# Nine row tiles for ACT instead of six, in longer bursts, in the plain aggregation runs of a graph network

## The reference

```
agg  = segment_sum((x @ weight[r])[edge_type, src], dst)          # layer 0
mean = segment_sum(x[src], dst) / max(deg, 1)                     # layer 1
out  = segment_sum(softmax_edges(...)[:, :, None] * feat[src], dst)   # layer 2, three times
out  = segment_sum(h[src] * (dinv[src] * dinv[dst])[:, None], dst)    # layer 3
```

## Time and profile before

| | |
|---|---|
| median of 3 runs | 6626.07 us (6622.88 to 6629.47) |
| profiled execution | 6623.83 us, its span 6622.0 us |
| PE, DVE, POOL, ACT busy | 71%, 68%, 69%, 44% of the span |
| plain runs in the span | a0 from 385 us, a1 from 1353 us, a5 from 5657 us to the end |

### The profile page before, as it was taken

One profiled execution on the slowest core, in us unless ns is written; L12 is line 12 of the kernel. 1 busy time (PEld: TensorE's weight loads), 2 busy tenths in 40 slices (PEclk: granted clock), 3 DMA queues, 4 the chain that ended last, 5 costly groups with the idle time before them and its releaser, 6 DMA issues. The chain is left out here.

```text
span 6622.0 us, 117574 instructions
## 1 busy us (share of the span) xinstructions
PE 4723.6 (71%) x16858; PEld 2807.9 (42%) x16858; DVE 4472.2 (68%) x11788; ACT 2887.8 (44%) x11591; POOL 4600.5 (69%) x4869
## 2 busy tenths in 40 slices
PE   9977777766777657767775777775677677666666
PEld 4445554543333334444443444443444444333333
DVE  5146566555555578888886888886888888655555
ACT  3310000000000067888875888885788888000000
POOL 0057777767777637777776777777777777677776
PEclk9988888878888877888887888787788877777777
DMA  6444444433333345555544555554555554344443
GB/s 204 160 138 122 123 123 122 122 107 109 109 109 109 106 143 141 142 143 144 141 118 135 142 142 146 142 141 148 139 142 141 142 144 118 102 116 116 117 116 106
DMA packets 446609, 865.78 MB, mean 131 GB/s; under 512 B 121901, under 2 KB 273094, under 8 KB 445866
## 3 DMA queue, kind: packets, MB, share of 16 engines
q0 software_dynamic: 227728, 627.54, 34.6%
q1 hardware_dynamic: 174624, 190.99, 9.1%
q10 hardware_dynamic: 43514, 39.73, 2.0%
HBM read 755.74 MB, written 102.10 MB: 130 GB/s over the span
## 5 line engine op out<-in xcount | busy, mean ns | idle before, releaser
L671 POOL DMA_INDIRECT rows_a<-table,rows_src x2454 | 2350.3, 958 | 882.5 <-issue 530.6
L891 PE MATMUL ps<-rows_a,hot_a 128*128 x4980 | 1858.6, 496 | 776.9 <-DMA rows_a<-table,rows_tile_a 407.6
L2064 ACT ACTIVATE rows_a<-rows_a,ex_a 128x64 f32<-128x64 f32 x9588 | 2321.1, 337 | 0.0
L2141 PE MATMUL ps<-rows_a,hot_a 128*128 128x260 f32 x4908 | 1814.3, 490 | 159.4 <-DVE agg L1973 145.9
L806 DVE TENSOR_TENSOR agg<-agg,ps 128x256 f32 (+1 forms) x2490 | 1045.6, 420 | 1202.4 <-PE ps L891 1130.3
L736 POOL DMA_INDIRECT rows_a<-table,rows_tile_a x1460 | 1383.5, 948 | 445.3 <-issue 257.8
L891 PEld LDWEIGHTS ps<-rows_a,hot_a 128*128 128x128 f32 x4980 | 1026.5, 236 | 1533.2 <-DVE agg L806 866.6
L1973 DVE TENSOR_TENSOR agg<-agg,ps 128x260 f32 x2490 | 1038.4, 417 | 319.0 <-PE ps L2141 130.4
L2141 PEld LDWEIGHTS ps<-rows_a,hot_a 128*128 128x128 f32 x4908 | 973.7, 230 | 449.2 <-issue 342.5
L736 POOL DMA_INDIRECT rows_a<-table,row x759 | 721.0, 950 | 231.6 <-issue 151.4
L2076 PE MATMUL ps<-ident,el_a 128*64 128x128 f32 x156 | 57.1, 366 | 520.1 <-DVE fac_a L1960 507.9
(11 more groups left out here) (355 smaller groups left out, 4165.3 us busy)
## 6 DMA issues: line engine op xcount, KB each, us to landing
rows_a<-table SPq DMA_DIRECT2D x6528, 1.0 KB
dstt_a<-dloc_dram SPq DMA_DIRECT2D x156, 512.0 KB
own_a<-table SPq DMA_DIRECT2D x4608, 1.0 KB
table<-ob SPq DMA_DIRECT2D x48, 1024.0 KB, 4.6
rows_a<-table,rows_src POOLq DMA_INDIRECT x2454
rows_a<-table ACTq DMA_DIRECT2D x2304, 1.0 KB
rows_a<-table,rows_tile_a POOLq DMA_INDIRECT x1460, 3.2
table<-ob_n SPq DMA_DIRECT2D x98, 130.0 KB, 3.0
```

The lines of the kernel that those rows point to most:

```text
L671: nc.gpsimd.indirect_dma_start(out=rows[:, n % ring, 0:width], out_offset=None, in_=table, in_offset=bass.IndirectOffsetOnAxis(ap=index[:, ...
L891: nc.tensor.matmul(ps[n % banks][:, 0:width], hot[:, m % nbuf, j, :], mine[n % 4], start=True, stop=True).then_inc(step_done, 1)
L2064: ins = nc.scalar.mul(a, a, ex[:, k % GV, s, h:h + 1])
L2141: nc.tensor.matmul(ps[j % banks][:, 0:W4], hot[:, j, :], step_rows(k, j), start=True, stop=True).then_inc(step_done, 1)
```

## The change

ACT takes every 86th tile from tile 78 on, which makes nine: 78, 164, 250, 336, 422, 508, 594, 680 and 766. Each is asked for in five bursts of 26, 26, 26, 25 and 25 rows. Three bursts stand ahead of the first block instead of four, and one follows each of the blocks 0 to 41. SP's requests for ACT's row numbers are placed by ACT's tile numbers. The constants also go into the step numbering, whose slices are cut from the first such tile on.

```diff
-ACT_TILE = 128
-ACT_FIRST = 100
+ACT_TILE = 86
+ACT_FIRST = 78
 ACT_TILES = tuple(range(ACT_FIRST, T - 1, ACT_TILE))
 ACT_PLACES = 2
-BURST = 16
-BURSTS_AHEAD = 4
+BURSTS = ((0, 26), (26, 52), (52, 78), (78, 103), (103, P))
+BURSTS_AHEAD = 3
...
-                        each = a[:, 0:n * stride].rearrange("p (i e) -> p i e", e=stride)
-                        nc.vector.tensor_scalar(own_tile[:, q, lo:lo + n], each[:, :, at:at + 1].rearrange("p i e -> p (i e)"),
+                        each = a[:, at:at + n * stride].rearrange("p (i e) -> p i e", e=stride)
+                        nc.vector.tensor_scalar(own_tile[:, q, lo:lo + n], each[:, :, 0:1].rearrange("p i e -> p (i e)"),
...
-                        sp.wait_ge(asked, P // BURST * (i - 1))
+                        sp.wait_ge(asked, len(BURSTS) * (i - 1))
...
-                    if ready < len(ACT_TILES) and i == (ACT_TILE * (ready - 1) + ACT_FIRST) // OWN_TILE - 1:
+                    if ready < len(ACT_TILES) and i == ACT_TILES[ready - 2] // OWN_TILE + 2:
...
-                bursts = iter(range(len(ACT_TILES) * P // BURST))
+                bursts = iter(range(len(ACT_TILES) * len(BURSTS)))
...
-                    i, lane = q * BURST // P, q * BURST % P
+                    i, (lane, end) = q // len(BURSTS), BURSTS[q % len(BURSTS)]
...
-                    ask_rows(act, mybir.EngineType.Activation, act_index[:, i % 2], lane, lane + BURST, BURST, octets, 4 * D,
+                    ask_rows(act, mybir.EngineType.Activation, act_index[:, i % 2], lane, end, end - lane, octets, 4 * D,
```

## The result

The changed kernel takes 6700.63 us (median of 5 runs, 6700.08 to 6707.59) against 6626.07 us: ratio 1.0118, 95% interval 1.0107 to 1.0129. It is 1.2% slower, where 0.17% faster was forecast and 6627 us was the end of the range.

What follows compares the result with a forecast made beforehand. POOL's issue of gathers was taken as the bound; 3 fewer gathers in each of three plain runs save 11.3 us, everything else costs nothing: 6626.1 - 11.3 = 6614.8 us, range 6608 to 6627.

Steps and rivals of the forecast that it cites:

- The gain, 11.3 us: POOL issues 3 fewer gathers in each of the three plain runs, each worth about 1.25 us: 11.3 us saved.
- Rival 3: Moved tiles bring nothing, since landings and not issues set the pace: 6626 us, chance 0.07.
- ten more register loads, 0.1 to 1.0 us: In each of ACT's longer bursts, loading ten more row numbers into registers adds 0.1 to 1.0 us.
- ACT's block: ACT's time per block with the new burst: 16.6 to 17.8, 18.6 to 19.6 and 19.0 to 20.0 us by run.
- POOL is reached only beyond ... 20.5 us a block: Ring allowance grows one step per block, so ACT's backlog holds up POOL only beyond 20.5 us a block.
- the last blocks give the backlog back: At a run's end, the last seven blocks, five before, have no burst and give ACT's backlog back.
- The head: ACT's upfront bursts of 78 rows take 3 to 5 us longer; covered by the ring, so no cost taken.
- rival 2: Part of the gain goes: POOL held up at t = 59 or second run ending late, 4 to 7 us; chance 0.14.
- The late number list: Second run, block 37: ACT stands 31 us for its last list of row numbers; nothing lost, bound 2 us.
- Rival 1: Slower: ACT's wait for its number list becomes the second run's end, blocks 37 to 48; 6636 us, chance 0.12.
- gaps over 0.3 us put down to PE: Sign of being wrong: POOL waiting on PE before gathers for longer than the forecast maximum of 0.3 us.
- a longer tail of the second run: Sign of being wrong: the second plain run's tail is longer than before.

Runs made afterwards that it cites:

- experiment 1: Changed kernel with bursts of 28, 28, 24, 24, 24 rows, so loads start on 16 bytes: 6624.46 us, ratio 0.9985 to the kernel before.
- experiment 2: Changed kernel, same bursts, ACT's loads of row numbers widened to start and end on 16 bytes: 6625.39 us, ratio 0.9985 to the kernel before.
- experiment 5: As experiment 1, with SP's requests for ACT's numbers one SP tile earlier: 6625.54 us, ratio 0.9984 to the kernel before.

## Why the prediction was wrong

**The gain, 11.3 us: right.** 3 x 3 gathers at 1.25 us. It shows in experiments 1 and 2 as 0.15% of 6635.54, 10 us, and no gap of POOL put down to PE passes 0.3 us in them. Rival 3, that the moved tiles bring nothing, falls with it.

**"ten more register loads, 0.1 to 1.0 us": the step that failed.** The ten are the numbers by which a load grew, from 16 to 25 or 26. I bounded them by nothing and by the whole gap of 1.5 us between bursts of 16 shared out over its 16 numbers, as if the number of registers were all. It measured 2.1 us in two bursts of five and 5.5 to 5.7 in three (a1), which is 0.9 and 4.3 to 4.5 us more than the 1.2 of before, 3.0 on average. The kernel before holds no load off 16 bytes: its starts are multiples of 16 numbers on ACT and of 32 on SP. Both ends of my bound were rows of the same kind, and the range was blind to the other. The borders 26, 78 and 103 stood in the diff. The Trainium skill, page "Runtime: NRT & Kernel Launch", section "Instruction fetch mechanics", gives about 200 ns a register, without a word on alignment. Its section "The ~15µs preamble/postamble breakdown" describes such loads as coming from HBM. The loads here come from SBUF, and agree with it only off 16 bytes (0.22 us).

**ACT's block, "19.0 to 20.0 us" in the last run and "16.6 to 17.8" in the first: too small.** Measured 21.3 and 20.7. The sum was also slightly off: its own terms give 19.1 to 20.3 us in the last run and 18.7 to 19.9 in the second (18.6 to 19.6 stood there). In a5 the load explains it: 5.6 us on average for 2.6, while the part between root and load was 6.8 us for the 7.7 of the block I read. In a0 the base was wrong as well: that part took 7.6 us on average and 6.4 in the one block I read, since ACT's waits for two of PE's products there grew from 1.2 and 1.6 us to 2.0 and 1.9; the load took 4.2 us for 1.2.

**"POOL is reached only beyond ... 20.5 us a block": roughly right, and not the edge that mattered.** POOL got gaps in a0 (20.7) and a5 (21.3), and none over 0.3 us in a1 (19.9). With two slow loads it had some 5 us of them already at 20.1 in a0 and 20.6 in a5. But the end of the run pays earlier, from 19.8 to 20.1 us: six intervals without a burst give back 11.0 us in place of 19.3 in a5, 50 us, and 12.6 in a0, 40 us, and the longer head has used some of that. I wrote that the last blocks give the backlog back and did not say up to which block length; that sum is the one to make. It comes close and no more: with the first root 3.0 us (a5) and 7.4 us (a0) later, it puts the edge at 20.4 and 20.1 us, 0.3 above what the table gives, and I can't place the rest.

**The head, "3 to 5 us longer": too small.** 78 rows took 34.0 to 34.5 us where 64 took 26.2, one of the three loads being slow. With good loads (experiment 2) they took 30.1 to 30.3, 4 us more, as forecast. "I take nothing" was not quite so: the first gaps of the changed kernel's a0 stand ahead of tiles 60 and 62, where the prediction looked for them (rival 2), but they exceed 0.3 us by 0.8 us together.

**The late number list, 31 us in the second run, "nothing lost": right, with the wait too long.** It is some 21 us in experiment 1 and 9.5 in the changed kernel, since longer blocks bring ACT there later; experiment 5 shows that it is free. (The count of the steps left was 4 short: 162 less four blocks of 17 are 94, not 90.)

**Rival 1** named the right engine and the right end: ACT becomes the end of the run. Its place (a1) and its cause (the list) were wrong. The chance of 0.12 was for these, so what came about had no chance of its own, and the range left both out. Of the two signs of being wrong, gaps over 0.3 us put down to PE came, and a longer tail of the second run did not.

## What to carry to other kernels

When work moves to an engine that "has room", add up its whole block, with every instruction that the new sizes change in form (start, length, alignment) and not only in count, and set it against the pace of the bound. A row of before bounds a new form only if it is of the same form. And where a queue has a backlog that a cheaper stretch pays back, work out the edge from the repayment: below it nothing shows, above it each us is paid once per block.

## What the runs showed of the hardware

A register load (TENSOR_LOAD) of consecutive 4-byte numbers from SBUF depends on where it starts. On ACT in a1, from a start at a multiple of four numbers: 1.2 us for 16, 1.7 for 24, 1.9 for 28, so 0.06 us a number and 0.24 on top; an odd end adds about 0.22 us for each number beyond the last full four (1.9 us for 25, 2.1 for 26), so 28 numbers load faster than 26. From any other start tried (17, 26, 49, 54, 75, 78, 102, 103, ...): 3.6 us for 16, 5.5 for 25, 5.7 for 26, 5.9 for 27, 0.22 to 0.23 us a number. Starts at 8 bytes but not 16 (26, 54, 78, 102) are as slow as the odd ones. Why was not tested. As a guess from these figures, 0.24 us for four more numbers from a good start and 0.22 for one from any other would fit fetches of four at once and of one. In a5, where the load follows an output DMA's request, the same loads take 1.2 to 1.5 us longer (medians of 3.5 and 6.9 to 7.0 us in the change, for 2.1 and 5.5 to 5.7), while the second load of a5's head, which follows none, took 5.8; that the request is the cause was not tested.
